# Second GAT projection as three fp16 matmuls, normalised values in PSUM, and a new fourteen-step order for a two-layer graph kernel

## The chip, the cores and the metric

The kernel runs on one core of a Trainium2 chip. The metric is the device time of one execution in microseconds (us), inputs and output in HBM; a verdict goes by the median of several executions. TensorE is called PE here, its weight loads PEld, VectorE DVE, ScalarE ACT, GpSimd POOL, and SyncE SP.

## The reference, cut to what matters

64 graphs of 128 nodes with 256 features go one by one through two attention layers.

```python
h = relu(layernorm(x))                       # x: (64, 128, 256)
# GAT layer 1: 4 heads of 128 features
xl = h @ W1                                  # 256 -> 512
e = leaky_relu(a_src[s] + a_dst[d]); e = where(mask, e, -1e9); attn = softmax over s
h = elu(attn^T @ xl + b1)                    # 128 x 512
# GAT layer 2: 1 head of 256 features
xl2 = h @ W2                                 # 512 -> 256, the "second projection"
x = x + attn2^T @ xl2 + b2
h = relu(layernorm(x))
# 8-head masked attention, 32 features each
q, k, v = h @ Wq, h @ Wk, h @ Wv
x = x + relu(softmax(mask(q k^T / sqrt(32))) @ v) @ Wo
```

## The kernel before

All weights stay in SBUF. The program is written once per engine: every engine runs its own list of functions, step after step. In step `t` a function with the lag `L` in its engine's list works on graph `t - L`, if there is one, so that up to twelve graphs are under way (`LAGS = 12`) and each engine touches most of them once in every step. The list is the order in which the engine does them, the lags are the stagger between graphs, and the engines meet at semaphores: `done(sem, g)` waits until the producer has finished graph g, `free` until the consumer has let go of a buffer with two halves, and `after(sem, g, lag)` until another graph has passed a point, which guards PSUM banks that several results share. `at_ends` is the same wait, made only for the first and the last `LAGS` graphs; `@once` marks work for graph 0 alone, such as the preparation of the weights. SP issues all loads, stores and the transposes made by DMA in an order of its own.

Most products are made "in three terms": a float32 operand is held as the sum of an fp16 high part and an fp16 low part, and high x high, high x low and low x high are added in PSUM (`SPLIT`, `split_matmul`, L928). Weights are first scaled by a power of two found from their largest element (`w1_row`, `w1_scale`, `proj_row`, `proj_scale` on DVE, with `turn_...` and `spread_...` on PE).

What the names of a step mean, in the order of a graph: `norm1_moments`, `variance1`, `rsqrt1` (POOL), `norm1_apply` (writes `z`), `relu1` (ACT, fp16 high part), `relu1_low` (DVE, low part), `norm1_transpose` (SP's DMA); `project1` (PE, L928 with `w_split,hT`); `ab_high`, `ab_low`, `xl_evac`; `transpose_ab`, `scores1_mask`, `scores1`; `gat1_leaky`, `gat1_scores`, `gat1_exp`, `gat1_recip`, `normalise` (POOL, L400), `transpose1`, `gat1_copy`, `aggregate1`, `elu_exp`, `elu` (DVE, L749, writes `h1T`); `project2` (PE, L954: float32 operands `h1T` and `w2`), `ab2_evac`, `xl2_evac`; `diagonal2`, `scores2`, ..., `aggregate2` (L1045); `residual1` (L830), `norm2_moments`, `variance2`, `rsqrt2` (POOL, L422), `norm2_apply`, `relu2`, `relu2_low`; `qk`, `project_v`, `scores3_...`, `mha_max`, `mha_exp_...`, `e3_..._halves` (POOL, L408 and L410), `mha_av` (L968 to L970), `att_norm` (L790), `att_copy`, `att_low` (L858), `project_out`, `residual2`, store.

Two places matter below. `project2` is one float32 product of 4 chunks; and `z` and `att` are float32 tiles in SBUF that DVE writes and that ACT and DVE read again:

```python
for k in range(H):
    ins = pe.matmul(X2[:, 0:D + 2], h1T[:, g.two, k * F:(k + 1) * F], w2[:, k, :], start=k == 0, stop=k == H - 1)
...
dve.scalar_tensor_tensor(out=z[:, g.two, which, :], in0=src, scalar=mv[:, g.two, which, 0:1],
                         in1=rstd[:, g.two, which:which + 1].to_broadcast((128, D)),
                         op0=ALU.subtract, op1=ALU.mult).then_inc(s[z_set], 1)
```

## Time and profile before

| | us |
|---|---|
| median of 3 runs (762.11 to 762.79) | 762.29 |
| the profiled execution's own time | 762.18 |
| its span (first to last instruction) | 760.3 |
| PE busy | 715.7 (94%) |
| DVE busy | 683.5 (90%) |
| ACT busy | 593.3 (78%) |
| POOL busy | 536.5 (71%) |

The profiled execution is one of the kernel's usual ones. PE's clock was granted in full in nearly the whole span. Because matmuls are pipelined, the duration of one overlaps the next: what a group costs PE is read from its start to the start of what follows it.

### The profile page before, as it was taken

The numbers are of one execution on the slowest core, as the hardware profiler recorded it, in microseconds if no ns is written. First come the engines' busy times: TensorE is split into PE (matmuls) and PEld (weight loads), VectorE is DVE, ScalarE is ACT, GpSimd is POOL, SyncE is SP. The second block draws the span as 40 slices with busy tenths as digits, with TensorE's granted clock in tenths as the row PEclk, the third lists the DMA queues.
The fourth block names the chain that finished last, engine by engine and source line by source line (L and its number), as shares of the span: only waits on it lengthen the run. The fifth ranks groups of instructions, "written<-read, shape, count | busy, mean of one in ns | idle before, by whom it ended". The sixth has DMA issues, their size and how long they took to land.

```text
span 760.3 us, 26536 instructions
## 1 busy us (share of the span) xinstructions
PE 715.7 (94%) x8398; PEld 592.9 (78%) x8398; DVE 683.5 (90%) x2017; ACT 593.3 (78%) x1865; POOL 536.5 (71%) x733
## 2 busy tenths in 40 slices
PE   0789999999999999999999999999999999999973
PEld 0477788888888888888888888888888888888852
DVE  5878999999999999999999999999999999999773
ACT  0468888788878888888888888888888888788852
POOL 7458777777677677767776777677777767776551
PEclk9999999999999999999999999999999999999995
DMA  6123466756567865676566566666657667555554
GB/s 204 38 54 67 99 119 110 120 112 125 105 119 114 121 113 116 116 116 114 119 119 111 119 115 122 105 121 117 121 110 120 113 123 109 117 114 91 99 106 103
DMA packets 270423, 84.70 MB, mean 111 GB/s; under 512 B 242896, under 2 KB 269904, under 8 KB 270288
## 3 DMA queue, kind: packets, MB, share of 16 engines
q1 hardware_dynamic: 269856, 82.24, 58.4%
q8 instruction: 70, 1.15, 0.6%
q10 hardware_dynamic: 432, 0.79, 0.4%
q14 instruction: 65, 0.53, 0.3%
HBM read 15.86 MB, written 8.39 MB: 32 GB/s over the span
## 4 chain that ended last, share of the span: by engine, by line
PE 78%; DVE 8%; DMA 4%; ACT 4%; issue 4%; SPq 1%; POOL 1%; DVEq 0%; ACTq 0%; POOLq 0%
PE bank L928 28%; PE bank L954 12%; PE bank L1104 7%; PE bank L1064 6%; PE bank L1083 4%; PE bank L1045 4%; PE bank L1053 3%; PE bank L980 3%; DMA hT<-h_split 3%; ACT e L554 2%; PE bank L1006 2%; PE bank L1004 2%; PE bank L996 2%; PE bank L970 1%; PE bank L969 1%
## 5 line engine op out<-in xcount | busy, mean ns | idle before, releaser
L554 ACT ACTIVATE e<-bank,nmx,q_power 128x128 f32<-128x128 f32 x512 | 194.5, 479 | 5.1 <-DVE nmx L853 4.9
L408 POOL CAST e_split<-e 128x512 f16<-128x512 f32 x128 | 89.7, 701 | 111.1 <-ACT e L554 111.1
L410 POOL TENSOR_TENSOR e_split<-e,e_split 128x512 f16<-128x512 f32 x128 | 152.1, 1188 | 10.3
L954 PE MATMUL bank<-w,h1T 128*128 128x258 f32 x512 | 122.5, 381 | 0.0
L422 POOL TENSOR_TENSOR rstd<-var,minus_half 128x1 f32<-128x1 f32 x128 | 71.7, 560 | 65.6 <-DVE var L718 65.6
L954 PEld LDWEIGHTS bank<-w,h1T 128*128 128x128 f32 x512 | 96.4, 190 | 15.7 <-DVE h1T L749 1.4
L928 PE MATMUL bank<-w_split,hT 128*128 128x260 f16 x768 | 98.0, 278 | 6.1 <-DVE w_split L649 4.9
L505 ACT ACTIVATE eT<-lr,nmx 128x128 f32<-128x128 f32 x256 | 102.6, 455 | 0.8 <-DVE nmx L805 0.8
L928 PE MATMUL bank<-h2T,proj_split 128*128 128x128 f16 x1536 | 96.2, 219 | 1.6 <-DMA h2T<-h_split 1.6
L928 PEld LDWEIGHTS bank<-h2T,proj_split 128*128 128x128 f16 x1536 | 91.0, 98 | 3.5 <-DMA h2T<-h_split 2.1
L928 PEld LDWEIGHTS bank<-w_split,hT 128*128 128x128 f16 x768 | 71.1, 98 | 17.3 <-DVE w_split L649 5.0
L481 ACT ACTIVATE h_split<-z 128x256 f16<-128x256 f32 x64 | 26.6, 416 | 71.4 <-DVE z L724 71.2
L848 DVE TENSOR_REDUCE top<-bank 128x8 f32<-128x1024 f32 x64 | 77.4, 1209 | 0.3 <-PE bank L1064 0.3
L1064 PEld LDWEIGHTS bank<-qkT 32*128 32x128 f16 x1536 | 42.9, 93 | 37.6 <-issue 36.0
L1104 PE MATMUL bank<-en,xl 128*128 128x128 f32 x512 | 68.3, 276 | 0.2
L400 POOL TENSOR_TENSOR eTn<-eT,rs 128x512 f32<-128x512 f32 x64 | 66.9, 1045 | 1.1 <-DVE rs L844 0.7
L1064 PE MATMUL bank<-qkT 32*128 32x128 f16 x1536 | 64.8, 216 | 0.3 <-DVE qkT L816 0.2
L505 ACT ACTIVATION_READ_ACCUMULATOR eT<-lr,nmx 128x1 f32 x256 | 64.9, 254 | 0.0
L1104 PEld LDWEIGHTS bank<-en,xl 128*128 128x128 f32 x512 | 62.2, 192 | 2.0 <-ACT en L512 1.3
L697 DVE SCALAR_TENSOR_TENSOR h_split<-z,h_split 128x256 f16<-128x256 f32 x128 | 59.6, 466 | 0.0
L724 DVE SCALAR_TENSOR_TENSOR z<-x_in,mv,rstd 128x256 f32<-128x256 f32 x64 | 59.1, 923 | 0.3 <-issue 0.3
L928 PE MATMUL bank<-proj_split,attT 128*128 128x256 f16 x384 | 54.3, 279 | 2.8 <-DMA attT<-att_split 2.8
(120 smaller groups left out, 1907.6 us busy)
## 6 DMA issues: line engine op xcount, KB each, us to landing
x_in<-in_x_dram SPq DMA_DIRECT2D x64, 128.0 KB, 2.3
out_dram<-x_out SPq DMA_DIRECT2D x64, 128.0 KB, 2.0
adj_in<-in_adj_dram SPq DMA_DIRECT2D x64, 64.0 KB, 2.4
e3T<-e_split SPq DMA_TRANSPOSE x128, 3.1
hT<-h_split SPq DMA_TRANSPOSE x64, 2.6
h2T<-h_split SPq DMA_TRANSPOSE x64, 2.5
attT<-att_split SPq DMA_TRANSPOSE x64, 2.6
w<-in_L_gnn_W_dram SPq DMA_DIRECT2D x2, 256.0 KB, 6.1
```

Of the source, the lines that this page charges most:

```text
L400: pool.tensor_tensor(eTn[:, g.two, :].rearrange("p (h n) -> p h n", h=H), eT[:, g.two, :].rearrange("p (h n) -> p h n", h=H), rs[:, g.two, ...
L408: pool.tensor_copy(e3_split[:, g.two, half, 0], e).then_inc(s[high_set], 1)
L410: pool.tensor_tensor(e3_split[:, g.two, half, 1], e, e3_split[:, g.two, half, 0], ALU.subtract).then_inc(s[low_set], 1)
L422: pool.tensor_tensor(rstd[:, g.two, which:which + 1], var[:, g.two, which:which + 1], minus_half[:, :], ALU.pow).then_inc(s[rstd_set], 1)
L505: ins = act.activation(eT[:, g.two, h * N:(h + 1) * N], lr[:, g.two, h * N:(h + 1) * N], ACT.Exp, bias=nmx[:, g.two, h:h + 1], accum_out=s ...
L554: ins = act.activation(e3[:, g.two, h, :], S[:, h // 4, (h % 4) * N:(h % 4 + 1) * N], ACT.Exp, bias=nmx3[:, g.two, h:h + 1], scale=q_power ...
L697: dve.scalar_tensor_tensor(out=out_, in0=in_, scalar=0.0, in1=high_, op0=ALU.max, op1=ALU.subtract).then_inc(s[sem_], 1)
L848: dve.tensor_reduce(top3[:, g.two, :], S.rearrange("p b (h n) -> p (b h) n", h=4), AX.X, ALU.max, negate=True).then_inc(s["top3_set"], 1)
L928: ins = pe.matmul(out_, left, right, start=n == 0, stop=n == len(pairs) - 1)
L954: ins = pe.matmul(X2[:, 0:D + 2], h1T[:, g.two, k * F:(k + 1) * F], w2[:, k, :], start=k == 0, stop=k == H - 1)
L1064: ins = pe.matmul(S[:, b, col * N:(col + 1) * N], qkT[r, g.two, i, h // 4, :], qkT[r, g.two, j, 2 + h // 4, :], start=False, stop=n == 2 a ...
L1104: ins = pe.matmul(O1[:, h * N:(h + 1) * N], xl[:, g.two, h * F:(h + 1) * F], en[:, g.two, h * N:(h + 1) * N], start=True, stop=True)
```

## The change

Three things are done together.

1. **The second projection in three fp16 terms.** `elu`'s result `h1T` is scaled by a power of two and split: `h1_high` (ACT, SBUF to SBUF, 128x512) and `h1_low` (POOL, 128x512) write `h1_split`; `w2` is scaled and split once (`w2_row`, `w2_scale` on DVE, `turn_w2` and `spread_w2` on PE); `project2` makes 12 fp16 matmuls. The scale is folded into `xl_evac`, `elu_exp`, `elu`, `ab2_evac` and `xl2_evac`, and `b1_prep` works it out in ten small DVE instructions.
2. **Normalised values in PSUM.** Both `norm..._apply` write into a bank of their own (`NORMED`, bank 7), as a `tensor_scalar` with mean and rstd as scalars in place of a `scalar_tensor_tensor` with rstd broadcast; `att_norm` works in place in the bank of `mha_av`; `relu...`, `att_copy` and the `..._low` functions read there.
3. **A new order** on all five engines with `LAGS = 14` and another map of the PSUM banks. `project1` goes from lag 3 to 5, `project2` from 5 to 7, `qk` from 7 to 10, `mha_av` from 9 to 11, `project_out` from 11 to 12, the store from 11 to 13.

```diff
-                for k in range(H):
-                    ins = pe.matmul(X2[:, 0:D + 2], h1T[:, g.two, k * F:(k + 1) * F], w2[:, k, :], start=k == 0, stop=k == H - 1)
-                ins.then_inc(s["x2_done"], 1)
+                split_matmul(X2[:, 0:D + 2], [
+                    [(h1_split[:, g.two, i, k * F:(k + 1) * F], w2_split[:, j, k, :]) for i, j in SPLIT] for k in range(H)]).then_inc(s["x2_done"], 1)
...
+            def h1_low(g):
+                done(pool, s["h1T_set"], g)
+                done(pool, s["h1_high"], g)
+                free(pool, s["x2_done"], g)
+                pool.tensor_tensor(h1_split[:, g.two, 1, :], h1T[:, g.two, :], h1_split[:, g.two, 0, :], ALU.subtract).then_inc(s["h1_low"], 1)
...
+            def h1_high(g):
+                done(act, s["h1T_set"], g)
+                free(act, s["x2_done"], g)
+                act.activation(h1_split[:, g.two, 0, :], h1T[:, g.two, :], ACT.Copy).then_inc(s["h1_high"], 1)
...
-                dve.scalar_tensor_tensor(out=z[:, g.two, which, :], in0=src, scalar=mv[:, g.two, which, 0:1],
-                                         in1=rstd[:, g.two, which:which + 1].to_broadcast((128, D)),
-                                         op0=ALU.subtract, op1=ALU.mult).then_inc(s[z_set], 1)
+                dve.tensor_scalar(NORMED[:, which, :], src, mv[:, g.two, which, 0:1], rstd[:, g.two, which:which + 1],
+                                  ALU.subtract, ALU.mult).then_inc(s[z_set], 1)
...
-                remainder(h_split[:, g.two, 1, :], z[:, g.two, 0, :], h_split[:, g.two, 0, :], "hT_set")
+                remainder(h_split[:, g.two, 1, :], NORMED[:, 0, :], h_split[:, g.two, 0, :], "hT_set")
...
-                dve.scalar_tensor_tensor(out=att[:, g.two, :].rearrange("p (h c) -> p h c", h=NH), in0=av[:, :, 0:DK], scalar=0.0,
+                dve.scalar_tensor_tensor(out=ATT[:, :, 0:DK], in0=ATT[:, :, 0:DK], scalar=0.0,
...
-                (scores3_mask, 8), (scores3_first, 8), (scores2, 6), (scores3_last, 8), (transpose_ab, 4), (transpose1, 5),
+                (qk, 10), (spread_w2, 7), (aggregate2, 9), (transpose_ab, 6), (scores1_mask, 6), (aggregate1, 7),
```

On PE, in a step of the middle of the program before, the float32 `project2` (L954) stands between `aggregate2` and `mha_av`, and `project1` follows:

```order
L1045 MATMUL bank<-xl,en 128x256
L954 MATMUL bank<-w,h1T 128x258 x4
L968 MATMUL bank<-vv,e3T 128x33
L969 MATMUL bank<-vv,e3T 128x32
L970 MATMUL bank<-vv,e3T 128x33
...
L928 MATMUL bank<-w_split,hT 128x260 x12
```

Of the change, the same stretch of PE (L1000 is `split_matmul`; `w_split,h_split` is `project2`, `w_split,hT` is `project1`):

```order
L1000 MATMUL bank<-w_split,hT 128x260 x12
L1041 MATMUL bank<-vv,e3T 128x33
...
L1000 MATMUL bank<-proj_split,attT 128x256 x6
L1000 MATMUL bank<-w_split,h_split 128x258 x12
L1105 MATMUL bank<-ident,eT 128x128
L1164 MATMUL bank<-ident,eTn 128x128 x4
L1000 MATMUL bank<-h2T,proj_split 128x128 x24
L1124 MATMUL bank<-xl,en 128x256
```

`project2` moved behind `project1`, `mha_av` and `project_out`; two transposes and `qk` stand between it and `aggregate2`.

On POOL, a step before ran from the masks (L437 to L440) through one pair of e halves, two rsqrt, the diagonal and `normalise` to the other pair:

```order
L437 TENSOR_SCALAR absent<-adj_in 128x128
L438 TENSOR_SCALAR mask_mha<-adj_in 128x128
L440 TENSOR_TENSOR mask_gat<-absent,offdiag 128x128
L408 CAST e_split<-e 128x512
L410 TENSOR_TENSOR e_split<-e,e_split 128x512
L422 TENSOR_TENSOR rstd<-var,minus_half 128x1 x2
L393 TENSOR_TENSOR diag<-ident,ab 128x128
L400 TENSOR_TENSOR eTn<-eT,rs 128x512
```

Of the change, POOL's step behind the e halves:

```order
L401 TENSOR_TENSOR diag<-ident,ab 128x128
L436 TENSOR_TENSOR rstd<-var,minus_half 128x1
L451 TENSOR_SCALAR absent<-adj_in 128x128
L452 TENSOR_SCALAR mask_mha<-adj_in 128x128
L454 TENSOR_TENSOR mask_gat<-absent,offdiag 128x128
L436 TENSOR_TENSOR rstd<-var,minus_half 128x1
L407 TENSOR_TENSOR h_split<-h1T,h_split 128x512
L414 TENSOR_TENSOR eTn<-eT,rs 128x512
```

The masks moved behind `rsqrt2` and ahead of `rsqrt1`, `h1_low` is new at L407, and `normalise` waits behind it.

## Rows read from the trace of the kernel before

**Rows 1.** Windows: stretch; its length; each engine's busy us (instructions); PEclk; DMA; GB/s

```profile
0.00:22.54 22.54, 0.93 (x3) 0.58 (x4) 13.67 (x30) 1.70 (x2) 15.96 (x29) 1.00 0.61 183
22.54:89.12 66.58, 61.71 (x534) 47.24 (x535) 55.99 (x167) 48.84 (x151) 43.34 (x60) 1.00 0.28 61
89.12:703.54 614.42, 612.84 (x7342) 514.79 (x7339) 579.25 (x1733) 512.92 (x1626) 451.86 (x616) 1.00 0.64 115
703.54:760.30 56.76, 40.26 (x532) 30.32 (x527) 34.54 (x91) 29.82 (x89) 25.34 (x30) 0.86 0.55 103
...
400.29:411.18 10.89, 10.89 (x132) 9.18 (x131) 10.17 (x32) 9.09 (x30) 7.87 (x11) 1.00 0.73 113
```

**Rows 2.** PE's timeline in one step: start us, us, engine, line, operation

```profile
400.29 0.38 PE L1004 MATMUL bank<-pick,abT 128*128 128x512 f16 x1
...
403.05 1.50 PE L928 MATMUL bank<-h2T,proj_split 128*128 128x128 f16 x24
404.38 0.65 PE L1045 MATMUL bank<-xl,en 128*128 128x256 f32 x2
404.87 1.91 PE L954 MATMUL bank<-w,h1T 128*128 128x258 f32 x8
406.62 0.18 PE L968 MATMUL bank<-vv,e3T 128*128 128x33 f16 x1
...
407.22 1.49 PE L928 MATMUL bank<-w_split,hT 128*128 128x260 f16 x12
408.55 0.59 PE L1053 MATMUL bank<-mask_mha,ident 128*128 128x512 bf16 x2
...
410.50 0.63 PE L1083 MATMUL bank<-ident,eTn 128*128 128x128 f32 x4
410.97 0.38 PE L996 MATMUL bank<-ident,mask_gat 128*128 128x512 f16 x1
411.18 0.38 PE L1004 MATMUL bank<-pick,abT 128*128 128x512 f16 x1
```

**Rows 3.** DVE's groups: busy us, mean ns of one, idle before and its releaser

```profile
L724 DVE SCALAR_TENSOR_TENSOR z<-x_in,mv,rstd 128x256 f32<-128x256 f32 x64 | 59.1, 923 | 0.3 <-issue 0.3
...
L724 DVE SCALAR_TENSOR_TENSOR z<-x,mv,rstd 128x256 f32<-128x256 f32 x64 | 31.4, 491 | 0.2
...
L858 DVE TENSOR_TENSOR att_split<-att,att_split 128x256 f16<-128x256 f32 x64 | 26.8, 418 | 0.6 <-ACT att_split L575 0.5
...
L822 DVE TENSOR_TENSOR vv<-bank,vv 128x256 f16<-128x256 f32 x64 | 26.3, 410 | 0.0
```

**Rows 4.** DVE's timeline in the same step

```profile
405.08 0.48 DVE L830 SCALAR_TENSOR_TENSOR x<-bank,rs,x_in 128x256 f32<-128x256 f32 x1 [0.42 <-PE bank L1045]
...
406.36 0.69 DVE L816 TENSOR_TENSOR qkT<-bank,qkT 128x512 f16<-128x512 f32 x1
...
408.13 0.98 DVE L724 SCALAR_TENSOR_TENSOR z<-x_in,mv,rstd 128x256 f32<-128x256 f32 x1
```

**Rows 5.** POOL's timeline in the same step

```profile
399.75 0.54 POOL L437 TENSOR_SCALAR absent<-adj_in 128x128 f32<-128x128 int32 x1
...
401.10 0.46 POOL L440 TENSOR_TENSOR mask_gat<-absent,offdiag 128x128 bf16<-128x128 f32 x1
...
407.80 1.03 POOL L400 TENSOR_TENSOR eTn<-eT,rs 128x512 f32<-128x512 f32 x1
```

**Rows 6.** POOL's and ACT's groups that resemble what is added

```profile
L410 POOL TENSOR_TENSOR e_split<-e,e_split 128x512 f16<-128x512 f32 x128 | 152.1, 1188 | 10.3
...
L422 POOL TENSOR_TENSOR rstd<-var,minus_half 128x1 f32<-128x1 f32 x128 | 71.7, 560 | 65.6 <-DVE var L718 65.6
...
L459 ACT ACTIVATE proj_split<-proj,scale 128x512 f16<-128x512 f32 x4 | 2.8, 709 | 0.0
```

**Rows 7.** DVE's timeline at the start: the first graph's `ab_high`

```profile
25.51 0.16 DVE L757 CAST ab_split<-bank 128x8 f16<-128x8 f32 x1
```

**Rows 8.** PE's timeline at the end: the last graph's `qk`

```profile
736.40 1.51 PE L928 MATMUL bank<-h2T,proj_split 128*128 128x128 f16 x24 [1.23 <-DMA h2T<-h_split]
```

More of the change, by code:

```diff
@@ L17 @@
+import math
 from contextlib import ExitStack
@@ L442, in _ @@
             steps(lambda graphs: run([
-                (e3_last_halves, 9), (split_low1, 6), (products_w2, 3), (masks, 3), (split_low2, 8), (split_low3, 9),
-                (picks, 0), (e3_first_halves, 8), (split_low0, 5), (products_w1, 1), (rsqrt1, 2), (rsqrt2, 6), (diagonal2, 5),
-                (normalise, 4),
+                (split_low3, 9), (picks, 5), (products_w2, 4), (e3_first_halves, 11), (split_low1, 7), (diagonal2, 8),
+                (products_w1, 3), (rsqrt2, 9), (masks, 5), (rsqrt1, 3), (split_low0, 6), (split_low2, 7), (h1_low, 7),
+                (normalise, 6), (e3_last_halves, 10),
             ], graphs))
@@ L480, in relu1 @@
                 wait(act, hT_here[g.two], g.dma2 - 16)
-                act.activation(h_split[:, g.two, 0, :], z[:, g.two, 0, :], ACT.Relu).then_inc(s["hT_high"], 1)
+                act.activation(h_split[:, g.two, 0, :], NORMED[:, 0, :], ACT.Relu).then_inc(s["hT_high"], 1)
             def gat1_leaky(g):
@@ L538, in relu2 @@
                 wait(act, h2T_here[g.two], g.dma2 - 16)
-                act.activation(h2_split[:, g.two, 0, :], z[:, g.two, 1, :], ACT.Relu).then_inc(s["h2T_high"], 1)
+                act.activation(h2_split[:, g.two, 0, :], NORMED[:, 1, :], ACT.Relu).then_inc(s["h2T_high"], 1)
             def qk_copy(g):
@@ L739, in norm1_apply @@
             def norm1_apply(g):
-                normed(g, 0, x_in[:, g.eight, :], "rstd_set", "hT_set", "z_set")
+                free(dve, s["hT_set"], g, 1)
+                after(dve, s["h2T_set"], g, -6)
+                normed(g, 0, x_in[:, g.eight, :], "rstd_set", "z_set")
             def ab_part(g, n):
@@ L747, in elu @@
                 done(dve, s["ex_set"], g)
-                free(dve, s["x2_done"], g)
-                dve.scalar_tensor_tensor(out=h1T[:, g.two, :], in0=ex[:, g.two, :], scalar=1.0, in1=O1[:, :],
+                free(dve, s["h1_high"], g)
+                free(dve, s["h1_low"], g)
+                dve.scalar_tensor_tensor(out=h1T[:, g.two, :], in0=ex[:, g.two, :], scalar=h1_scale[:, 0:1], in1=O1[:, :],
                                          op0=ALU.min, op1=ALU.max).then_inc(s["h1T_set"], 1)
@@ L838, in norm2_apply @@
             def norm2_apply(g):
-                normed(g, 1, x1[:, g.eight, :], "rstd2_set", "h2T_set", "z2_set")
+                free(dve, s["h2T_set"], g, 1)
+                after(dve, s["hT_set"], g, 5)
+                normed(g, 1, x1[:, g.eight, :], "rstd2_set", "z2_set")
             def gat1_recip(g):
@@ L984, in transpose_ab @@
                 done(pe, s["ab_set"], g)
[L985 removed]
+                after(pe, s["en2_set"], g, -3)
                 at_ends(pe, s["abT_set"], g, -1)
[L987 removed]
+                at_ends(pe, s["ab_set"], g, 0)
+                at_ends(pe, s["xl_set"], g, 0)
                 pe.transpose(ABT, ab_split[:, g.two, :], ident16[:, :]).then_inc(s["abt_done"], 1)
@@ L1089, in project_out @@
                 pe.wait_ge(attT_here[g.two], g.dma2)
-                after(pe, s["ab_set"], g, 7)
-                after(pe, s["xl_set"], g, 7)
+                after(pe, s["qkT_set"], g, 2)
                 at_ends(pe, s["x_out_set"], g, -1)
+                after_once(pe, power_set["w1"], g, 11)
                 split_matmul(WO[:, 0:D], [
@@ L1107, in _ @@
             steps(lambda graphs: run([
-                (scores3_mask, 8), (scores3_first, 8), (scores2, 6), (scores3_last, 8), (transpose_ab, 4), (transpose1, 5),
-                (turn_w1, 0), (scores1_mask, 4), (scores1, 4), (project_out, 11), (turn_proj, 4), (spread_proj, 4),
-                (spread_w1, 3), (aggregate1, 5), (w2_ones, 5), (transpose2, 6), (project_v, 8), (qk, 7), (aggregate2, 6),
-                (project2, 5), (mha_av, 9), (project1, 3),
+                (qk, 10), (spread_w2, 7), (aggregate2, 9), (transpose_ab, 6), (scores1_mask, 6), (aggregate1, 7),
+                (spread_proj, 6), (scores1, 6), (scores3_mask, 10), (scores2, 8), (w2_ones, 7), (scores3_first, 10),
+                (project_v, 10), (scores3_last, 10), (project1, 5), (mha_av, 11), (spread_w1, 1), (project_out, 12),
+                (turn_w2, 6), (project2, 7), (turn_w1, 0), (turn_proj, 4), (transpose2, 8), (transpose1, 6),
             ], graphs))
```

234 lines of the change are left out of this document (146 added, 88 removed).

## Prediction

> **What bounds the kernel now.** I read the windows first, because they separate the pipelined middle from its ends, then the timelines of one step, then the groups of the operations that the change touches.
>
> The windows are cut at the first `project1` (22.54), the eighth (89.12) and the last (703.54) [rows 1]. From the eighth to the last PE is busy 612.84 of 614.42 us. It waits for nobody there, while DVE has 579.25, ACT 512.92 and POOL 451.86. 56 steps in 614.42 us are 10.97 us a step. The step looked at closely runs from 400.29 to 411.18, 10.89 us, all of it PE [rows 1, 2]; the 0.08 between the two numbers are small irregularities, which I leave in. At the ends it is otherwise: 22.54 us before the first `project1`, seven ramp steps in 66.58 us, and 56.76 us behind the start of the last one, where a graph's own chain sets the time [rows 1]. So a gain has to come off PE's step, and it counts only until another engine's work, or a loop through several engines, is longer than PE's.
>
> The span is 760.30 and the execution's time 762.18, 1.88 more; the median of the runs is 762.29, 0.11 above that execution.
>
> **Project2, the PE term.** Four float32 products (eight rows of 258 columns) start at 404.87 and `mha_av` starts at 406.62: 1.75 us [rows 2]. The new form is that of `project1`: 12 fp16 matmuls of 260 columns from 407.22 to 408.55, 1.33 us, 0.111 each. With 258 columns that is 1.32. Saved: 0.43 a step. No other PE work changes in the steady part, so PE's step becomes 10.46, or 10.97 - 0.43 = 10.54 with the irregularities. Over the 56 steps: -24.1 us. In the ramps PE is not the bound, so I do not count it there.
>
> **DVE.** Its step is busy 10.17 of 10.89 [rows 1]. Two operations shrink. `z<-x_in` has a mean of 923 ns and `z<-x`, the same shape and form, 491 [rows 3]. The longer one starts at 408.13, while POOL is in `normalise` from 407.80 for 1.03 us, and ends with 0.98 at 409.11, 0.28 behind POOL's [rows 4, 5]: two tiles are read in SBUF by both, and one waits for the other. The new instruction reads one tile and writes PSUM. No row has DVE writing PSUM; the nearest of 256 elements are 410 (PSUM in) and 418 (SBUF in) [rows 3], and the bounds are 410 and the 923 of today (nothing gained). I take 430, because the collision needs the second tile and the size alone gives 410. That is -0.49 and -0.06. The rest turns nearly even: `xl2_evac` becomes a `scalar_tensor_tensor` (+0.06), the others keep count and size. DVE: 10.17 - 0.49 = 9.68 busy, plus waits that no order takes away (0.42 before `residual1` today [rows 4]), so about 10.1 of 10.46. If nothing shrinks: 10.17 + 0.42 + 0.06 = 10.65, and DVE is the bound by 0.19.
>
> The Trainium skill ("SBUF — State Buffer", Who interferes with whom) says that a Vector instruction with two SBUF inputs is kept out while a GpSimd one reads SBUF, and that one with a single SBUF input, outside the two-port modes, is not. By that rule the new form is free of POOL everywhere, which is the 410 end; the traces of `z` agree, 923 against 491. Against the change, its page "VectorE: DVE Perf Modes" (The TRN2 errata) charges a PSUM source 62 cycles at 0.96 GHz more than an SBUF one, 65 ns, for three reads that move to PSUM: an estimate of 0.2 us a step more on DVE. The pair 410 and 418 shows none of it.
>
> **ACT.** `h1_high` is added, 128x512 from SBUF to fp16: 709 ns by L459 [rows 6]; its neighbours overlap it by about a tenth, so 0.61 to 0.71. 9.09 + 0.65 = 9.74 busy of 10.46. It lies between `gat2_leaky` and `relu2`, where `exp` of two graphs follows. Cover left: 0.7 us, less the waits; about 0.4.
>
> **POOL.** `h1_low` is added, 1188 ns by L410, which has the same shapes [rows 6]. 7.87 + 1.19 = 9.06 of 10.46; it can lose 0.2 to 0.3 if the collisions with DVE go.
>
> **The tightest wait.** In the new order `project2` waits for `h1_low`, and POOL does that behind `rsqrt2`, the three masks and `rsqrt1`; `rsqrt2` waits for DVE's `variance2`, and that for `aggregate2`. The chain from the end of `aggregate2`: `residual1`, moments and the gaps to the start of `qk_low`, 1.28 (405.08 to 406.36), `qk_low` 0.69 [rows 4], `variance2` and hand-overs 0.4 (my estimate from the gaps there), `rsqrt2` 0.56 [rows 6], masks 1.81 (399.75 to 401.56) [rows 5], `rsqrt1` 0.56, `h1_low` 1.19 [rows 6]: 6.5 us. PE's own work between the same points is the step without `qk` 1.33, `aggregate2` 0.49, `project2` 1.32, `transpose1` 0.47 [rows 2] and the small `transpose2` 0.11 (an estimate, half of two 128-column rows of `transpose1`): 10.46 - 3.72 = 6.74. It fits with 0.2 to spare.
>
> **The start.** `project1` of graph 0 still waits for the split `w1`, about 0.7 us later (norm work stands ahead of it): 23.2. Then DVE has `b1_prep` at 2.5 us (two 128x512 passes at some 0.45, a reduce at 0.7, seven tiny ones near 0.15, all estimates from the sizes in [rows 3]) before `ab_high` of graph 0, which stood at 25.51 [rows 7] and comes near 29. `w2`'s reductions and split (some 4 us) stand ahead of the first `elu`. I put graph 2's `project1` 4 us and the first `project2` 9 us later than now. But the ramp is one step shorter: `project_out` follows `project1` by 7 steps and not 8, and its first steps hold less. Ramp steps are chains of 7 to 8 us, from `aggregate1` through `h1_low`, `normalise` and back, and the eighth `project1` comes at 87 to 91; I take 89, as now (89.12). Term: 0, bounds -2 and +6.
>
> **The end.** The last `qk` starts 32.9 us after the last `project1` and 23.9 before the end [rows 1, 8]. It now comes 5 steps after and not 4, but they are emptier: about 33 to 34; behind it `project_v` stands between the halves of the scores, +0.7. Term: +1.7, bounds 0 and +5.
>
> **Sum.** 760.3 - 24.1 + 0 + 1.7 = 737.9 span; + 1.9 + 0.1 = 739.9 as a median if nothing slips. Four more steps lie in the stretch with extra waits at the ends, and the loops above are within 0.4 of PE: I add 1 us for them and forecast 741.
>
> **The rivals.**
> *Another engine takes over, the gain is cut.* DVE at 10.65 plus 0.08 makes -0.24 a step in place of -0.43: 56 x 0.19 = 10.6 more, 752. It happens if writing PSUM is dear (above some 600 ns each) or if `z` is still held up; the same price stands for ACT if its loop is 0.5 longer than I count. For it: three engines between 9.7 and 10.1 of 10.46. Against: today DVE runs at 93% beside a PE that never waits. Chance 0.18.
> *The start and the end eat more.* Both at their bounds, +6 and +3.3: 750. For it: w2's preparation on the engine that is the busiest then. Chance 0.10.
> *Slower: `project2` waits for `h1_low` in every step.* Once that chain is more than 0.24 longer than 6.5, each tenth beyond costs 0.1 x 56 = 5.6 us; the gain is gone at 0.43 more, so the point is a chain of 7.2. If POOL's masks and `h1_low` were stretched by a fifth (3.0 x 0.2 = 0.6) and each hand-over cost 0.1 more (five of them), the chain would be 7.6, the step 11.3 and the time 741 + 0.86 x 56 = 789; with half of it 761 to 765. For it: masks ahead of a critical subtraction; against: POOL's durations are steady, and the collisions get fewer. Chance 0.09.
> *The PE saving is not there:* float32 and fp16 rows cost as in [rows 2] or not at all; I see no reason, 0.01.
> The forecast, PE still the bound at 10.45 to 10.6: 0.62.
>
> **How the numbers follow.** 741 is the likeliest case, whose own range is 736 to 747. The range 735 to 754 takes in the first two rivals and leaves out the slower one and the far part of the first. A change within 0.2% (1.5 us) is about what this kernel's measurement cannot tell from none. Faster: 0.62 + 0.17 + 0.10 and a little of the third, 0.90; same 0.02; slower 0.08.
>
> **What would show it.** Right: PE busy over 99% in the middle with a step of 10.46; `w_split,h_split` from its start to the next row 1.32; `NORMED` near 0.43 in both forms; `h1_high` 0.65 to 0.71; the eighth `project1` near 89. Wrong: PE idle ahead of the new `project2` with `h1_low` as its releaser; DVE without gaps and PE waiting on `x1_set`, `xl_set` or `qkT_set`; a `z` row still above 600 ns; the first `mha_av` much later than in the trace of before.

## The result and the profile after

The change leaves the time nearly where it was: 763.39 us as the median of 14 runs (760.14 to 764.53) against 762.05 of the kernel before (14 runs), ratio 1.0018, 95% interval 1.0010 to 1.0025. That is slower by 0.18%, small but outside the noise. The forecast was 741, with a range of 735 to 754. The profiled execution took 763.64, its span is 761.9.

The windows of the trace after, cut at the same places and with the same columns as [rows 1] (first, eighth and last `project1`, end), and one step:

```profile
0.00:26.68 26.68, 1.09 (x5) 0.73 (x6) 18.17 (x35) 1.67 (x2) 16.01 (x28) 1.00 0.54 162
26.68:94.44 67.76, 55.35 (x498) 42.48 (x497) 56.26 (x178) 47.55 (x141) 43.51 (x62) 1.00 0.26 55
94.44:688.47 594.03, 587.54 (x7564) 494.59 (x7561) 565.20 (x1724) 536.76 (x1681) 488.13 (x672) 1.00 0.63 119
688.47:761.90 73.43, 45.35 (x600) 35.09 (x596) 38.00 (x103) 35.97 (x109) 30.09 (x37) 0.81 0.48 82
402.92:413.40 10.48, 10.48 (x140) 8.74 (x136) 10.17 (x32) 9.62 (x31) 8.73 (x12) 1.00 0.67 139
```

The middle is 20.4 us shorter (594.03 against 614.42). The eighth `project1` comes 5.3 later (94.44), and what lies behind the last one is 16.7 longer (73.43 against 56.76). PE tells the same in another way: its busy time fell by 26.4 (715.7 to 689.3), and its idle time grew by 28.0, from 44.6 to 72.6. By parts, window less busy, the idle time went from 21.6 to 25.6, from 4.9 to 12.4, from 1.6 to 6.5, and at the end from 16.5 to 28.1. So the work was saved, and it was paid back in waits: 4.9 us of them in the middle, the rest at the two ends.

PE's timeline in that step (it answers to [rows 2]; L1000 is `split_matmul`, `w_split,h_split` is `project2`):

```profile
402.92 1.50 PE L1000 MATMUL bank<-w_split,hT 128*128 128x260 f16 x12
404.86 0.82 PE L1000 MATMUL bank<-proj_split,attT 128*128 128x256 f16 x6
405.58 1.49 PE L1000 MATMUL bank<-w_split,h_split 128*128 128x258 f16 x12
406.90 0.27 PE L1105 MATMUL bank<-ident,eT 128*128 128x128 f32 x1
```

`project2` goes from 405.58 to 406.90: 1.32, the value forecast.

The groups that answer to [rows 3] and [rows 6]:

```profile
L424 POOL TENSOR_TENSOR e_split<-e,e_split 128x512 f16<-128x512 f32 x128 | 148.5, 1160 | 10.3
L407 POOL TENSOR_TENSOR h_split<-h1T,h_split 128x512 f16<-128x512 f32 x64 | 74.3, 1160 | 6.2 <-ACT h_split L538 4.3 <-DVE h1T L806 1.9
L538 ACT ACTIVATE h_split<-h1T 128x512 f16<-128x512 f32 x64 | 40.3, 630 | 0.5 <-DVE h1T L806 0.5
L806 DVE SCALAR_TENSOR_TENSOR h1T<-ex,h_scale,bank 128x512 f32<-128x512 f32 x64 | 47.8, 747 | 8.9 <-ACT ex L533 6.8
L779 DVE TENSOR_SCALAR bank<-x,mv,rstd 128x256 f32<-128x256 f32 x64 | 34.8, 544 | 1.7 <-POOL rstd L436 1.5
L779 DVE TENSOR_SCALAR bank<-x_in,mv,rstd 128x256 f32<-128x256 f32 x64 | 34.5, 539 | 0.0
L838 DVE SCALAR_TENSOR_TENSOR xl<-bank,x_power,b_all 128x256 f32<-128x256 f32 x64 | 30.4, 475 | 0.2 <-issue 0.2
L846 DVE SCALAR_TENSOR_TENSOR bank<-bank,rs 128x256 f32<-128x256 f32 x64 | 27.7, 433 | 2.2
L916 DVE TENSOR_TENSOR att_split<-bank,att_split 128x256 f16<-128x256 f32 x64 | 26.6, 416 | 5.9 <-ACT att_split L596 5.7
```

PE's waits between 110 and 680 us (line waited for, us in total, times, longest):

```profile
PE bank L1000 <- DMA attT<-att_split: 5.4, 13, 0.9
```

A regular step takes 10.48 to 10.50, but where `project_out` waits for the transposed `att` it is longer (up to 11.2), and the mean is 594.03 / 56 = 10.61.

The start, PE's waits between 24 and 50 us (L960 is `turn_proj`, L974 `turn_w2`, L1064 `transpose_ab`):

```profile
PE bank L960 <- DVE largest L697: 9.3, 1, 9.3
PE bank L974 <- DVE largest L722: 2.3, 1, 2.3
PE bank L1064 <- DVE ab_split L818: 1.8, 1, 1.8
```

The end: the starts of `qk` behind the last `project1` (they answer to [rows 8]), first after, then the first three of the four before:

```profile
692.95 1.50 PE L1000 MATMUL bank<-h2T,proj_split 128*128 128x128 f16 x24
703.23 1.50 PE L1000 MATMUL bank<-h2T,proj_split 128*128 128x128 f16 x24
714.60 1.50 PE L1000 MATMUL bank<-h2T,proj_split 128*128 128x128 f16 x24
723.41 1.50 PE L1000 MATMUL bank<-h2T,proj_split 128*128 128x128 f16 x24 [1.01 <-DMA h2T<-h_split]
735.32 2.58 PE L1000 MATMUL bank<-h2T,proj_split 128*128 128x128 f16 x24 [0.62 <-issue]
```

```profile
710.23 1.50 PE L928 MATMUL bank<-h2T,proj_split 128*128 128x128 f16 x24
719.38 1.50 PE L928 MATMUL bank<-h2T,proj_split 128*128 128x128 f16 x24
727.70 1.51 PE L928 MATMUL bank<-h2T,proj_split 128*128 128x128 f16 x24 [0.33 <-DMA h2T<-h_split]
```

The last steps do not get shorter as graphs run out: from 692.95 to 735.32 four of them take 42.4 us, 10.6 each. In the kernel before they did: the three from 710.23 to 736.40 take 26.2, 8.7 each. The last `qk` is 46.9 behind the last `project1` (32.9 before) and 26.6 ahead of the end (23.9 before). So of the 16.7 us, 14.0 lie ahead of the last `qk` and 2.7 behind it. With 8.7 a step, five steps in place of four would have put the last `qk` at 4.5 + 4 x 8.7 = 39.4 behind the last `project1`, 6.5 later than before (an estimate from these rows); the other 7.5 are the longer steps. The chain of what ended last, in order of time (start, us, what), shows what the steps consist of:

```profile
720.54 1.23 DVE top L906
...
723.10 0.47 ACT e L575
...
723.63 0.61 POOL e_split L422
...
724.32 1.15 POOL e_split L424
725.47 0.56 POOL e_split L422
...
726.11 1.17 POOL e_split L424
727.29 5.21 DMA e3T<-e_split
...
732.55 0.21 PE bank L1041
...
735.32 2.60 PE bank L1000 x24
737.93 0.61 ACT qkT L565
738.56 0.70 DVE qkT L872
...
741.06 1.24 DVE top L906
```

From one maximum (`mha_max`, L906) to the one two graphs later are 20.5 us: exps, four passes of e halves on POOL, the transpose, `mha_av` (L1041), `qk` of the next step, its copy and low part, and the scores. In the kernel before the same view is a nearly unbroken line of PE work up to 725, 35 us before its end; here most of it lies outside PE from 686 on, 76 us before the end.

### The profile page after: what moved, and what is told of

It is laid out like the page before. It is cut to its first block and busy times, and to the rows that moved or that the text cites. A ratio compares the mean times of both kernels' runs of the same rounds, so it can differ in the third digit from the quotient of the medians.

```text
span 761.9 us, 27375 instructions
## 1 busy us (share of the span) xinstructions
PE 689.3 (90%) x8657; PEld 572.9 (75%) x8657; DVE 677.6 (89%) x2037; ACT 621.9 (82%) x1929; POOL 577.8 (76%) x796
## 5 line engine op out<-in xcount | busy, mean ns | idle before, releaser
L575 ACT ACTIVATE e<-bank,nmx,q_power 128x128 f32<-128x128 f32 x512 | 185.8, 468 | 13.0 <-DVE nmx L911 9.8
L424 POOL TENSOR_TENSOR e_split<-e,e_split 128x512 f16<-128x512 f32 x128 | 148.5, 1160 | 10.3
L1000 PE MATMUL bank<-w_split,hT 128*128 128x260 f16 x768 | 98.8, 279 | 2.3 <-issue 2.2
L519 ACT ACTIVATE eT<-lr,nmx 128x128 f32<-128x128 f32 x256 | 99.2, 392 | 0.1
L1000 PE MATMUL bank<-w_split,h_split 128*128 128x258 f16 x768 | 95.7, 273 | 3.6 <-POOL h_split L407 1.9
L1000 PE MATMUL bank<-h2T,proj_split 128*128 128x128 f16 x1536 | 97.3, 220 | 1.7 <-DMA h2T<-h_split 1.0
L1000 PEld LDWEIGHTS bank<-h2T,proj_split 128*128 128x128 f16 x1536 | 90.7, 98 | 4.4 <-DMA h2T<-h_split 1.9
L422 POOL CAST e_split<-e 128x512 f16<-128x512 f32 x128 | 78.2, 611 | 20.5 <-ACT e L575 19.2
L1000 PEld LDWEIGHTS bank<-w_split,h_split 128*128 128x128 f16 x768 | 72.5, 97 | 18.5 <-issue 7.4
L1000 PEld LDWEIGHTS bank<-w_split,hT 128*128 128x128 f16 x768 | 70.8, 99 | 19.1 <-issue 2.6
L906 DVE TENSOR_REDUCE top<-bank 128x8 f32<-128x1024 f32 x64 | 77.8, 1215 | 1.8 <-PE bank L1145 1.8
L407 POOL TENSOR_TENSOR h_split<-h1T,h_split 128x512 f16<-128x512 f32 x64 | 74.3, 1160 | 6.2 <-ACT h_split L538 4.3
L533 ACT ACTIVATE ex<-bank,exp_shift,h_unscale 128x512 f32<-128x512 f32 x64 | 49.9, 779 | 27.6 <-PE bank L1184 27.6
L1000 PE MATMUL bank<-proj_split,attT 128*128 128x256 f16 x384 | 55.0, 281 | 10.1 <-DMA attT<-att_split 9.8
L1145 PEld LDWEIGHTS bank<-qkT 32*128 32x128 f16 x1536 | 43.0, 93 | 26.4 <-issue 22.9
L1041 PE MATMUL bank<-vv,e3T 128*128 128x33 f16 x512 | 45.7, 179 | 16.2 <-DMA e3T<-e_split 16.1
L806 DVE SCALAR_TENSOR_TENSOR h1T<-ex,h_scale,bank 128x512 f32<-128x512 f32 x64 | 47.8, 747 | 8.9 <-ACT ex L533 6.8
```

The source lines that it names most:

```text
L407: pool.tensor_tensor(h1_split[:, g.two, 1, :], h1T[:, g.two, :], h1_split[:, g.two, 0, :], ALU.subtract).then_inc(s["h1_low"], 1)
L422: pool.tensor_copy(e3_split[:, g.two, half, 0], e).then_inc(s[high_set], 1)
L424: pool.tensor_tensor(e3_split[:, g.two, half, 1], e, e3_split[:, g.two, half, 0], ALU.subtract).then_inc(s[low_set], 1)
L519: ins = act.activation(eT[:, g.two, h * N:(h + 1) * N], lr[:, g.two, h * N:(h + 1) * N], ACT.Exp, bias=nmx[:, g.two, h:h + 1], accum_out=s ...
L533: act.activation(ex[:, g.two, :], O1[:, :], ACT.Exp, bias=exp_shift[:, :], scale=h1_unscale[:, 0:1]).then_inc(s["ex_set"], 1)
L575: ins = act.activation(e3[:, g.two, h, :], S[:, h // 4, (h % 4) * N:(h % 4 + 1) * N], ACT.Exp, bias=nmx3[:, g.two, h:h + 1], scale=q_power ...
```

## The experiments

Times are medians, and ratios are to the kernel before, measured beside each run. "Tail" is the time from the last `project1` to the end of the span: 56.76 before, 73.43 after. It comes from the one profiled execution of a run, which can lie off the median: by 3.1 us in e6, and by 1.3 to 2.0 in e1, e2, e5, e14 and e16. So a difference of a microsecond or two between tails says little.

**One part alone: the order.** `e9_order_alone` keeps the order, the lags and the bank map of the change, with the arithmetic of the kernel before: `project2` is the float32 product, `h1_high`, `h1_low` and the preparation are gone, and the normalised values go to SBUF. `att_norm` still works in PSUM.

```diff
-                split_matmul(X2[:, 0:D + 2], [
-                    [(h1_split[:, g.two, i, k * F:(k + 1) * F], w2_split[:, j, k, :]) for i, j in SPLIT] for k in range(H)]).then_inc(s["x2_done"], 1)
+                for k in range(H):
+                    ins = pe.matmul(X2[:, 0:D + 2], h1T[:, g.two, k * F:(k + 1) * F], w2[:, k, :], start=k == 0, stop=k == H - 1)
+                ins.then_inc(s["x2_done"], 1)
...
-                (elu_exp, 7), (gat1_leaky, 6), (gat2_leaky, 8), (split_high3, 7), (split_high0, 6), (h1_high, 7), (relu2, 9),
+                (elu_exp, 7), (gat1_leaky, 6), (gat2_leaky, 8), (split_high3, 7), (split_high0, 6), (relu2, 9),
```

> The new order and bank map alone: project2 is the float32 product again, h1_high and h1_low are gone, the scale of h1 is the constant 1 (no b1 bound, no largest, row, scale, turn or spread for w2, no w2 split), and the normalised values go to SBUF as before. It is the arithmetic of the kernel before in the order of the change. If the order itself makes the start and the end longer: the middle is PE's 10.89 to 10.97 a step as before, the part behind the last project1 is 70 to 73 us (56.8 before), the total 772 to 777. If what was lost belongs to the new work (preparation of w2 and b1, the two h1 passes in every loop): the ends are as before and the total is 760 to 764.

778.65 us, ratio 1.0223 (1.0204 to 1.0241). Its windows, cut in the same way:

```profile
27.21:92.95 65.74, 54.92 (x475) 43.47 (x475) 50.00 (x160) 44.92 (x134) 38.90 (x57) 0.95 0.27 55
92.95:705.20 612.25, 607.38 (x7340) 514.51 (x7336) 567.82 (x1725) 513.56 (x1625) 456.03 (x616) 1.00 0.59 116
705.20:776.20 71.00, 47.56 (x588) 36.72 (x584) 37.91 (x103) 35.04 (x107) 26.91 (x34) 0.82 0.46 85
```

Its last `qk`:

```profile
750.76 2.72 PE L989 MATMUL bank<-h2T,proj_split 128*128 128x128 f16 x24 [1.87 <-DMA h2T<-h_split]
```

| part | forecast | measured | order alone | the rest of the change |
|---|---|---|---|---|
| to the eighth `project1` | 0 | +5.3 | +3.8 | +1.5 |
| middle | -24.1 | -20.4 | -2.2 | -18.2 |
| tail | +1.7 | +16.7 | +14.2 | +2.4 |

The order by itself costs 16 us and nearly all of it in the tail. The first theory of the expectation holds; the total is 1.7 us above its range. The last `qk` is 45.6 behind the last `project1`, and its chain of what ended last leaves PE at 705.4, 71 us before the end. PE's float32 product is back here, so the longer tail does not need the shorter PE step.

**Without the preparation.** `e10_no_prep` sets the scale of h1 to 1 and leaves out the bound on b1 and the search for w2's largest element.

```diff
+            pool.memset(h1_scale[:, :], 1.0).then_inc(s["h1_scale_set"], 1)
...
-                dve.tensor_reduce(h1_bound[:, 0:1], b1_all[:, :], AX.X, ALU.max, apply_absolute_value=True).then_inc(s["b1_largest"], 1)
...
-                powers_of_two("w2", 6, 8)
```

> The change as made, without the preparation: the scale of h1 is the constant 1, b1 is not bounded or scaled, w2 is split unscaled with no search for its largest element (two reductions, w2_row, powers of two, turn_w2 and spread_w2 left out; the two split passes stay). If the preparation is what makes the first eight steps longer: the eighth project1 comes at 88 to 91 in place of 94.4, total 757 to 760. If the ramp is set by its own loops through h1_low and normalise: 93 to 94 and 762 to 763.

759.24 us, 0.9964 (0.9950 to 0.9979). The eighth `project1` comes at 91.64, 2.8 earlier than in the change, and the tail is 71.85, 1.6 shorter. So the preparation is over half of the 5.3 at the start. The 3.8 of e9 and these 2.8 cannot be added: e9 leaves the preparation out as well, has the longer `project2`, and PE did not run equally fast in the first 45 us. The second `project1` took 1.49 in e9, 2.8 in the change and 2.4 in e10, and it takes 1.49 at the full clock. (The PEclk column shows 1.00 for the change there; these durations are those of half the clock.) What the order alone costs at the start is therefore not settled.

**The start's order.** `e15_start` moves `picks` to POOL's step 0, `proj_largest` behind `ab_low` and `turn_proj` behind the first `project1`. `e18_start_b1` also puts `b1_prep` behind `ab_high`, and has the matmuls of e17 (below) at the end.

```diff
-                (split_low3, 9), (picks, 5), (products_w2, 4), (e3_first_halves, 11), (split_low1, 7), (diagonal2, 8),
+                (split_low3, 9), (picks, 0), (products_w2, 4), (e3_first_halves, 11), (split_low1, 7), (diagonal2, 8),
...
-                (w1_largest, 0), (ab_low, 5), (att_norm, 11), (residual2, 12),
+                (w1_largest, 0), (ab_low, 5), (proj_largest, 5), (att_norm, 11), (residual2, 12),
```

> Only the start: picks go back to POOL's step 0, where they stood before; proj_largest on DVE goes behind ab_low of graph 0, and turn_proj on PE behind the first project1. If the wait of PE for proj_largest and the picks beside the split of w1 are what makes the first project1 late: it starts at 22.6 to 24.5 in place of 26.7, the eighth at 91 to 93 in place of 94.4, total 760 to 762. If the ramp is set by the preparation on DVE anyway: first project1 earlier, the eighth at 94, 763.

> The edits of e15 and of the run before this, and b1_prep on DVE behind ab_high of graph 0 and no longer ahead of it. If what is left at the start (eighth project1 at 93.7 with e15's edits) comes from b1_prep standing ahead of ab_high: 91.5 to 92.5, and the total is that of the run before this less 2 to 3. If it comes from w2's preparation two steps later: 93.5, and only e15's 0.7 is gained.

e15: 762.37, 1.0009 (0.9998 to 1.0021). The first `project1` starts at 23.24, as forecast for this edit, 3.4 earlier; the eighth at 93.73, only 0.7 earlier. e18: 761.34, 1.0003 (0.9988 to 1.0017), and the eighth is later again, at 94.97; the expected 2 to 3 us did not come, and it is 1.1 slower than e17. The wait of PE for `proj_largest` was visible and nearly free. That DVE's work behind it sets the ramp is the second theory of the expectation and fits; no run varied it by itself. Of the preparation, moving `b1_prep` gives nothing; which of w2's pieces costs the 2.8 was not taken apart.

**The values in SBUF again.** `e12_z_sbuf` undoes the second part of the change for the normalised values; `att` stays in PSUM.

```diff
-                dve.tensor_scalar(NORMED[:, which, :], src, mv[:, g.two, which, 0:1], rstd[:, g.two, which:which + 1],
-                                  ALU.subtract, ALU.mult).then_inc(s[z_set], 1)
+                dve.scalar_tensor_tensor(out=z[:, g.two, which, :], in0=src, scalar=mv[:, g.two, which, 0:1],
+                                         in1=rstd[:, g.two, which:which + 1].to_broadcast((128, D)),
+                                         op0=ALU.subtract, op1=ALU.mult).then_inc(s[z_set], 1)
```

> The change as made, but the normalised values go to SBUF again, by the old instruction with two SBUF inputs. If it is what keeps DVE below PE: the x_in form costs 0.9 us in place of 0.55, DVE is busy 10.3 to 10.5 of a step and sets it at 10.7 to 10.9, total 775 to 785. If PE has slack left: 763 to 767.

781.63, 1.0257 (1.0237 to 1.0277): the expected size, for the most part by another mechanism. Its groups:

```profile
L780 DVE SCALAR_TENSOR_TENSOR z<-x_in,mv,rstd 128x256 f32<-128x256 f32 x64 | 32.2, 503 | 0.0
L780 DVE SCALAR_TENSOR_TENSOR z<-x,mv,rstd 128x256 f32<-128x256 f32 x64 | 30.8, 482 | 1.7 <-POOL rstd L437 1.5
L425 POOL TENSOR_TENSOR e_split<-e,e_split 128x512 f16<-128x512 f32 x128 | 169.3, 1323 | 10.3
L455 POOL TENSOR_TENSOR mask_gat<-absent,offdiag 128x128 bf16<-128x128 f32 x64 | 38.1, 595 | 4.0
```

On DVE the old form is the shorter one (503 and 482 against 539 and 544). POOL pays: its subtraction takes 1323 ns in place of 1160, and POOL is busy 33.6 us more in the middle (521.74 against 488.13, 56 steps in both). DVE pays too, in other instructions: the low part of the normalised values takes 491 in place of 410 and `nmx<-top,q_power` 586 in place of 449, and DVE is busy 11.7 us more in the middle. The regular step is 10.70. Between 110 and 680 us PE waits 8.2 us for the transposed e halves, which POOL's subtraction feeds and for which it never waits there in the change, and 1.9 for `vv` of DVE. So the PSUM bank is what lets the middle run at PE's pace, more through POOL than through DVE.

**PE's order.** `e11_swap` puts `project_out` behind `project2`.

```diff
-                (project_v, 10), (scores3_last, 10), (project1, 5), (mha_av, 11), (spread_w1, 1), (project_out, 12),
-                (turn_w2, 6), (project2, 7), (turn_w1, 0), (turn_proj, 4), (transpose2, 8), (transpose1, 6),
+                (project_v, 10), (scores3_last, 10), (project1, 5), (mha_av, 11), (spread_w1, 1), (turn_w2, 6),
+                (project2, 7), (project_out, 12), (turn_w1, 0), (turn_proj, 4), (transpose2, 8), (transpose1, 6),
```

> Only PE's order: project_out stands behind project2 and no longer ahead of it, 1.3 us later in the step, so that the transposed att has landed. If the attT waits (5.4 us in the middle) are what makes the mean step 10.61 where the regular one is 10.49: middle 588 to 590 in place of 594, total 757 to 760. Rival: residual2 is then late for the bank it shares with qk, qk waits in every step for x_out, 0.1 to 0.5 us a step, 766 to 790.

810.35, 1.0637 (1.0621 to 1.0653), with a step of 11.40. Its waits of PE between 110 and 680:

```profile
PE bank L1000 <- DVE vv L878: 20.4, 36, 0.6
PE bank L1000 <- POOL h_split L407: 7.8, 14, 0.6
```

The attT waits are gone, and `project2`, 0.72 earlier in the step, waits for `vv_set` (they share bank 3) and for `h1_low`. The reserve of `project2` is smaller than 0.72. The rival came as well, too small for the list of waits: in the step at 402 us `qk` starts 0.72 behind `transpose1` (0.46 in the change), at 408.06, right behind the `x_out` that DVE ends at 407.91. Of the 0.92 that a step is longer, that is about 0.26.

**SP's order.** `e3_sp_order` issues the att transpose ahead of the second e3 transpose; `e4_tail59_sp` has e1's edit as well.

```diff
-                (e3_transpose_last, 11), (e3_transpose_first, 11), (att_transpose, 12),
+                (e3_transpose_last, 11), (att_transpose, 12), (e3_transpose_first, 11),
```

> The changed kernel with one swap in SP's list: the attention output's transpose (att_transpose) stands ahead of the second e3 transpose instead of behind it. In the middle PE waits ahead of project_out for that transfer in 13 steps of about 54, 5.4 us in total, and steps of 10.8 to 11.4 us stand among those of 10.49. Theory M1 (the transfer is queued behind the e3 ones): these waits go, the mean step falls from 10.61 to about 10.52, and 3 to 5 us are saved: 758 to 760. [...]

> Both together: five graphs of the end one step later, and SP's swap. If theories A and M1 hold and the two stretches are apart, the savings add: 12 to 15 us, 748 to 751. With A alone 753 to 756, with M1 alone 758 to 760.

e3: 770.64, 1.0109 (1.0092 to 1.0126), over 10 us above the forecast of its first theory; e4: 769.63, 1.0109 (1.0094 to 1.0124). In e3 the wait has changed its place and doubled:

```profile
PE bank L1041 <- DMA e3T<-e_split: 10.3, 12, 1.6
```

**Moving mha_av in the last steps.** e1 does `mha_av` and all that follows it, up to the store, one step later for graphs 59 to 63 (`LATE_FROM = 59`), e2 for 62 and 63 (62). e5 moves `mha_av` of 59 to 61 right behind `qk` of the next step, and the att functions behind it. e6 gives the result of `aggregate2` of graphs 61 to 63 a bank of its own, e7 also puts `gat2_copy` ahead of the exps, and e8 is e5 and e7 together.

```diff
+LATE_FROM = 59
...
+MOVED = {'mha_av': ('qk', 12), 'att_norm': ('norm2_apply', 12), 'att_low': ('gat2_scores', 12), 'att_copy': ('gat2_leaky', 12)}
...
+        O2_OF = lambda g: bank[:, 0] if g.n >= 61 else bank[:, 5]
```

> The changed kernel, in which the last five graphs (59 to 63) take mha_av, att_norm, att_copy, att_low, att_transpose, project_out, residual2 and the store one step later; nothing else moves. Theory A (the end is a ring: scores3 of a graph, maximum, exp, e halves, two DMA transposes, mha_av, and behind it on PE qk and scores3 of the graph after next; about 20.7 us for two steps whatever else is left): the ring then spans three steps, the steps of the end fall from 10.4 to about 7 us, and 8 to 11 us are saved: 753 to 756. Theory B (the two e3 transposes back to back on SP, landing 4.4 to 5.2 us later in place of 3.1, set the end): they stay as they are, each graph still waits for them, so at most 1 to 2 us are saved, or the extra step costs some: 761 to 768.

> As the run before, for the last two graphs only (62 and 63). Theory A: only the last one or two rounds of the ring are cut, so 2 to 5 us are saved, a third to a half of the five-graph version: 758.5 to 761.5. Theory B: no change within 1.5 us, 762 to 765.

> Only the last steps are changed: mha_av of graphs 59, 60 and 61 is issued right behind qk of the next step (one step later), with att_norm, att_low and att_copy moved after it; nothing of the first 58 graphs. Theory A (the end is set by the loop scores3, maximum, exp, e halves, transpose, mha_av, then qk of the next step, because PE stands at mha_av and cannot start qk): the waits at mha_av of 1.9 and 3.0 us leave the path, the last qk comes 2 to 5 us earlier after the last project1 than the 46.8 us of the change as made, total 759 to 762. Theory B (the end is set by the loop scores3, exps, gat2_copy, aggregate2, residual1, scores3_mask): nothing is gained, 763 to 765, since PE then waits for x1 at scores3_mask instead.

> Only graphs 61 to 63: the result of aggregate2 gets a PSUM bank that nothing else uses by then, so it needs not wait until the exps of the scores have read the shared bank, and scores3 need not wait for residual1 either. Order unchanged. Theory B (the shared bank closes the loop): 1 to 3 us less than the change as made, whose steps at the end are 8.8 to 11.9 us. But gat2_copy still stands behind the exps on ACT, so if that place in ACT's list is what counts, nothing is gained (0 to 1 us). Theory A: nothing, 763 to 764.5.

> As the one before, and gat2_copy of graphs 62 and 63 is done on ACT ahead of the two halves of the softmax's exps (as in the kernel before), where it otherwise waits 2.9 us behind them. Theory B: the loop of 8.5 to 8.8 us becomes 6 to 7, the last two steps shrink, and the total is 757 to 760. Theory A (mha_av's wait for its transposed operand sets the steps): 762 to 764.

> Both sets of moves together. If both loops take turns, neither alone gives much (0 to 2 us each) and together they give 5 to 8 us: 755 to 758, faster than both kernels. If one loop alone sets the end, this run equals the better one of the single edits within 1 us.

| run | us | ratio, interval | tail |
|---|---|---|---|
| e1 | 768.67 | 1.0096, 1.0081 to 1.0112 | 76.58 |
| e2 | 764.54 | 1.0034, 1.0021 to 1.0046 | 72.31 |
| e5 | 767.42 | 1.0083, 1.0070 to 1.0096 | 77.75 |
| e6 | 762.64 | 1.0018, 1.0004 to 1.0031 | 73.95 |
| e7 | 768.08 | 1.0088, 1.0075 to 1.0102 | 77.11 |
| e8 | 768.81 | 1.0110, 1.0089 to 1.0130 | 78.47 |

None helps: all but e6 lie above the change's own 1.0018, and e6 equals it. e1 does bring the last `qk` 3.2 us closer to the last `project1`, but what lies behind it grows by 6.4, and PE waits there for the att chain:

```profile
PE bank L1005 <- DMA attT<-att_split: 13.4, 5, 4.3
PE bank L1046 <- DVE att_split L921: 4.8, 2, 3.8
```

Theory B as e5 to e7 have it, the loop through the shared bank, falls with e6 (nothing gained) and e7 (8 us and more above its forecast). Of theory A, what falls with e1 and e5 is that moving `mha_av` cuts the loop; the loop itself comes back below as theory C. In e1 the wait that was removed came back at another place.

**Shortening the loop instead.** `e13_low_out` leaves the low half of e3 out for graphs 58 to 63, 2.3 us on POOL per graph, and moves nothing. `e14_low_dve` gives half of it to DVE and leaves nothing out; `e16_start_low_dve` is e14 with e15.

```diff
+                if g.n >= 58:
+                    pool.tensor_tensor(e3_split[:, g.two, half, 1, 0:1, 0:1], e[:, 0:1, 0:1], e3_split[:, g.two, half, 0, 0:1, 0:1],
+                                       ALU.subtract).then_inc(s[low_set], 1)
...
+                    dve.tensor_tensor(e3_split[:, g.two, 1, 1], e3[:, g.two, 4:8, :], e3_split[:, g.two, 1, 0], ALU.subtract).then_inc(s["e3_low_last"], 1)
```

> Ablation at the end only: for graphs 58 to 63 the low half of e3 is left out (one element is subtracted in place of 128x512, twice per graph; the transposes and everything else stay). Theory C (behind the last project1 the steps are set by the loop scores3, maximum, exps, e halves on POOL, transpose, mha_av, qk of the next step, 20.9 us for two steps, which holds two of these subtractions of 1.16 us each): each pass is 2.3 us shorter, the last qk comes 4 to 6 us earlier behind the last project1 than 46.8, and the last pass gives 2.3 more; total 755 to 758. Rival (the steps there are set by the work of PE or by residual1 and scores3_mask): only the last pass gets shorter, 761 to 762.

> The same loop shortened without leaving anything out: for graphs 58 to 63 the low half of the last four heads is computed by DVE, behind att_low, while POOL goes on with the first four heads. Theory C: POOL's chain is 1.2 us shorter in every pass, 2 to 4 us in all, total 759 to 761. If DVE's work behind it (residual1, norm2) is delayed by as much as is saved: 763 to 765.

> The two edits before this together. If start and end are independent, their gains add: 756 to 759, 0.3 to 0.8% less than the kernel before the change.

e13: 758.15, 0.9958 (0.9945 to 0.9971). The window of its tail, 5.9 shorter than the change's:

```profile
688.97:756.50 67.53, 43.74 (x600) 33.63 (x596) 38.05 (x103) 35.78 (x109) 18.85 (x37) 0.86 0.45 89
```

The last `qk` starts at 731.77, 42.8 behind the last `project1` and 4.05 closer than in the change, and the rest lies behind it. The rival (only the last pass) gave 2.3. So POOL's passes are on the path of the last steps, and theory C holds at this place. e14: 767.00, 1.0072 (1.0057 to 1.0086); e16: 765.43, 1.0047 (1.0032 to 1.0062), where 756 to 759 were expected. Their tails are 75.35 and 74.42. DVE is busy 4 us more there, and it is a queue of the same loop; that this is why they got longer is argued, not shown.

**PE kept busy.** `e17_keep_busy` puts 56 matmuls that nobody reads where PE waits at the end.

```diff
+                if g.n in (61, 63):
+                    keep_busy(34 if g.n == 63 else 10)
...
+                if g.n == 63:
+                    keep_busy(12)
```

> As the change, with PE kept busy where it waits at the very end: fp16 matmuls of 512 columns into a bank that nothing uses any more, 10 ahead of mha_av of graph 61, 34 ahead of mha_av of graph 63 (7.2 us of a wait of 9.95) and 12 ahead of the last project_out (2.5 of 3.2). They write nothing that is read. If half the granted clock at the end is part of the loss: qk of graph 63 takes 1.5 us in place of 2.6, the last project_out 0.83 in place of 1.46, and the clock behind the last project1 is 0.95 and more in place of 0.81; total 760.5 to 762. If the loop through POOL and the transposes hides PE's clock: the clock is full and the total unchanged, 763 to 764.

760.27, 0.9974 (0.9963 to 0.9985). Tail and last `qk`:

```profile
688.57:759.10 70.53, 56.94 (x656) 40.12 (x652) 38.31 (x103) 36.01 (x109) 30.03 (x37) 0.92 0.45 85
```

```profile
734.53 1.50 PE L1000 MATMUL bank<-h2T,proj_split 128*128 128x128 f16 x24 [0.62 <-issue]
```

The last `qk` takes 1.50 in place of 2.58, the last `project_out` 0.83 in place of 1.46, and the tail is 2.9 shorter. Its clock is 0.92, below the 0.95 that was expected: it still fell between 720 and 730 us, and the `qk` ahead of the last one took 2.40. This is the one version with all of the work in it that is faster than both kernels, by 0.26% against the kernel before.

## Why the prediction was wrong

In the terms of the sum, the span came out 24.0 us above 737.9: 3.7 in the middle, 5.3 at the start and 15.0 at the end.

**The PE term** was right. Project2 takes the 1.32 forecast; the regular step is 10.48 (10.46 forecast). The mean missed by 0.07 a step, 3.7 us in all: the waits for `attT` (5.4 us in total) took the place of the irregularities that I carried over from before.

**The DVE term** failed without harm. I had 9.68 busy, and the step shows 10.17, as before. That one step hides a gain of half the size forecast: the mean over the middle fell from 579.25 / 56 = 10.34 to 565.20 / 56 = 10.09, 0.25 and not 0.49. `NORMED` costs 0.54 and not 0.43 for `x_in` as for `x`. Three instructions that got a scalar from a tile grew by 59 to 67 ns (`h1T` to 747 from 688, `xl2` to 475 from 411, `ab2` to 218 from 151), where I had counted 0.06 for one of them. I also had the others keep their size: `nmx<-top,q_power` grew from 310 to 449 with the same operands, and the low part of the normalised values shrank from 466 to 410. The new `NORMED` takes two such scalars: 410 and two times 64 is 538, what it measured. Writing PSUM is not what costs, since `att_norm` in place in PSUM (L846) takes 433. That reading comes from comparing rows; no run varied the scalars by themselves, and in two of the three the form of the instruction changed as well. The mechanism was only half right: I put the whole collision on DVE. The Trainium skill ("SBUF — State Buffer", Who interferes with whom) says that a Vector instruction with two SBUF inputs contends with a GpSimd one that reads SBUF, and that the order in which they are issued decides which of the two is held up. The traces fit that: DVE paid in [rows 3], 923 against 491, and in the new order the same form shows 503 and 482, and POOL's subtraction is longer by 163 ns (e12). The charge for a PSUM source in "VectorE: DVE Perf Modes" of the Trainium skill (The TRN2 errata) shows in no row here: `att_low` read SBUF before, 418, and reads PSUM now, 416.

**ACT and POOL** were right: `h1_high` 0.63 (0.61 to 0.71), `h1_low` 1.16 (1.19); 9.62 and 8.73 busy, against 9.74 and 9.06 less the few tenths.

**The tightest wait** was right: PE never waits for `h1_low` in the middle, and e11 shows that 0.72 less is too little. The rivals that it and the other engines stood for did not come. (The price "with half of it 761 to 765" is off at its lower end: half of what was added to the chain makes 7.05, a step of 10.77 and 758.)

**The start, term 0**, failed by 5.3, inside the bounds of -2 and +6. I had the first `project1` 0.7 later and it is 4.1 later (26.68 against 22.54), behind `turn_proj`; but e15 took back 3.4 of that and won 0.7. I counted 4 to 9 us of delays for graphs 0 and 2 and let a shorter ramp give them all back; it gave back a part. The runs put 2.8 on the preparation (e10); where the other 2.5 come from stays open.

**The end, term +1.7**, is the step that failed: 16.7, far outside 0 and +5. "It now comes 5 steps after and not 4, but they are emptier: about 33 to 34" took the length of the last steps from PE's work. The last `qk` came at 46.9. For 33 to 34 the four steps behind the first `qk` would have had to take about 7.3 each; they took 8.7 in the order before and 10.6 now. They are emptier (PE idle 28.1 of 73.4) and still take that long, because the loop of `scores3` through POOL and the transposes to `mha_av` and `qk` takes 20.5 for two steps, most of it outside PE. I checked one wait of the new order against the step (the 6.5 of 6.74), found it just short enough, and did not ask of the other loops how long a step they allow when PE's own work runs out. 14.2 of the 16.7 come with the order alone (e9), and e13 shows that the loop's length counts. The full clock gives 2.9 back (e17); the kernel before also ended at half the clock, so how much of the 16.7 is clock was not measured, and these shares overlap. Which pieces make the loop longer than in the order before, beyond `qk` standing between `mha_av` and the scores, is not settled: none of the edits that moved one of them (e1 to e8) made the kernel faster. Of the rivals, "the start and the end eat more", with its 0.10, is the one that came, at 20.3 us above the forecast terms in place of 9.3.

## What to carry to other kernels

A software pipeline can have loops through several engines that are just short enough for the full step. Here such a loop set the length of the last steps, once the bottleneck engine ran empty. A sum of saved work per step is only the middle: price the tail as the number of steps behind the last first-stage operation, times the step that the longest loop allows, and look whether the chain that ended last leaves the bottleneck engine earlier. Removing or moving a wait gained nothing in the eight runs e1 to e8. Leaving out work that was part of it did (e13), and so did faster PE work (e17); handing work to another engine of the same loop did not (e14).
